# A GNN kernel on one core: the sum of a graph's two slot sums made by POOL in SBUF instead of by two accumulating transposes on TensorE

## What is computed

```python
h = jnp.maximum(_layernorm(x, axis=-1), 0.0)
mask = (adj > 0.0)
h_pair = relu((h @ W1a)[:, :, None, :] + (h[:, :, None, :] - h[:, None, :, :]) @ W1b + b1)   # 192 wide
hm = einsum('bjkh,bjk->bjh', h_pair, mask)
x = x + hm @ W2 + deg[..., None] * b2
h = jnp.maximum(_layernorm(x, axis=-1), 0.0)
x = x + einsum('bno,...->bno', einsum('bnm,bmf->bnf', adj, h), W)
```

## Time and profile before

| | |
|---|---|
| median of 3 runs | 842.6 us (842.23, 842.6, 845.79) |
| the profiled execution | 845.98 us |
| its span, first to last instruction | 844.1 us |
| mean granted TensorE clock | 0.98 |
| PE busy | 810.6 us (96%) |
| DVE busy | 809.9 us (96%) |
| ACT busy | 794.9 us (94%) |
| POOL busy | 611.5 us (72%) |

### The profile page before, as it was taken

How to read it: one execution, slowest core, us unless ns; L and a number is a source line. 1 busy time by engine, 2 the same in 40 slices (tenths; PEclk the granted TensorE clock), 3 DMA queues, 4 the chain that set the end, 5 groups by cost and what they waited for, 6 DMA issues and landing times.

```text
span 844.1 us, 26648 instructions
## 1 busy us (share of the span) xinstructions
PE 810.6 (96%) x8242; PEld 715.0 (85%) x8243; DVE 809.9 (96%) x2894; ACT 794.9 (94%) x2246; POOL 611.5 (72%) x1174
## 2 busy tenths in 40 slices
PE   4879999999999999999999999999999999999996
PEld 2447888898889888988998899888988898889884
DVE  6969999999999999999999999999999999999993
ACT  4969999999999999999999999999999999999992
POOL 1966777777777777777777777777777777777762
PEclk8979999999999999999999999999999999999996
DMA  9800000000000000000000000000000000000000
GB/s 337 327 1 2 7 9 21 21 21 15 21 20 21 9 21 21 20 15 21 21 21 9 20 21 21 15 21 20 21 9 21 21 20 14 21 21 21 15 3 21
DMA packets 26705, 27.55 MB, mean 33 GB/s; under 512 B 3520, under 2 KB 24512, under 8 KB 25536
## 3 DMA queue, kind: packets, MB, share of 16 engines
q1 hardware_dynamic: 25488, 25.37, 8.9%
q10 hardware_dynamic: 1072, 0.43, 0.2%
HBM read 21.59 MB, written 4.19 MB: 31 GB/s over the span
## 4 chain that ended last, share of the span: by engine, by line
PE 90%; DVE 4%; issue 2%; ACT 2%; DMA 1%; SPq 0%; ACTq 0%; DVEq 0%
PE ring L414 48%; PE ring L442 8%; PE prep L471 5%; PE post L514 4%; PE post L501 3%; PE post L508 3%; PE post L502 3%; PE prep L479 3%; PE prep L482 2%; PE prep L477 2%; DVE acc L826 2%; PE post L506 2%; DMA x_all<-x_nbf_dram 1%; PE prep L473 1%; DVE onehot_space L812 1%
## 5 line engine op out<-in xcount | busy, mean ns | idle before, releaser
L826 DVE SCALAR_TENSOR_TENSOR acc<-ring,acc 128x384 f32<-128x384 f32 x896 | 488.6, 545 | 0.6
L572 ACT COPY ring<-P 128x384 f32<-128x384 f32 x1024 | 466.6, 509 | 19.3 <-DVE acc L826 11.4
L414 PE MATMUL ring<-PQ,onehot_space 128*128 128x192 f16 x4096 | 417.0, 247 | 4.5 <-ACT ring L572 2.2
L414 PEld LDWEIGHTS ring<-PQ,onehot_space 128*128 128x128 f16 x4096 | 328.0, 99 | 39.4 <-issue 13.5
L922 POOL TENSOR_SCALAR start<-P,spare 128x192 f32<-128x192 f32 x128 | 128.4, 1003 | 134.8 <-ACT P L622 133.8
L946 POOL TENSOR_TENSOR row_space<-row_space 128x192 f32<-128x192 f32 x256 | 153.4, 599 | 25.3 <-ACT row_space L610 8.2
L812 DVE TENSOR_SCALAR onehot_space<-mask_all 128x512 f16<-128x512 f16 x512 | 158.1, 311 | 0.0
L442 PE MATMUL ring<-PQ,owner 128*128 128x384 f16 (+1 forms) x512 | 93.9, 306 | 0.0
L414 PE MATMUL ring<-PQ,onehot_row 128*128 128x192 f16 x768 | 84.3, 246 | 0.5 <-DVE onehot_row L874 0.3
L610 ACT ACTIVATE row_space<-ring 128x576 f32<-128x576 f32 x128 | 83.3, 651 | 0.7 <-PE ring L414 0.7
L826 DVE SCALAR_TENSOR_TENSOR acc<-ring,start 128x384 f32<-128x384 f32 x128 | 71.1, 556 | 5.3 <-PE ring L414 1.3
(11 more groups left out here) (138 smaller groups left out, 1431.9 us busy)
## 6 DMA issues: line engine op xcount, KB each, us to landing
onehot_space<-adj_kbj_dram SPq DMA_DIRECT2D x8, 1024.0 KB, 17.3
adj_again<-adj_kbj_dram SPq DMA_DIRECT2D x128, 64.0 KB, 2.0
x_all<-x_nbf_dram SPq DMA_DIRECT2D x8, 512.0 KB, 19.0
out_dram<-x_all SPq DMA_DIRECT2D x32, 128.0 KB, 1.9
consts<-consts_dram SPq DMA_DIRECT2D x1, 192.0 KB, 2.4
scratch<-w1a_dram ACTq DMA_DIRECT2D x2, 48.0 KB, 4.2
scratch<-w1b_dram ACTq DMA_DIRECT2D x2, 48.0 KB, 6.7
scratch<-b_dram ACTq DMA_DIRECT2D x1, 96.0 KB, 10.1
```

The lines of the kernel that those rows point to most:

```text
L414: last = nc.tensor.matmul(to, hot(s), parts[:, part, H:2 * H], start=False, stop=(part == 1), skip_group_check=True)
L572: return nc.scalar.copy(slots[to][:, bank_], src.unsqueeze(1).broadcast_to([N, PER_BANK, H]))
L826: return nc.vector.scalar_tensor_tensor(sums, slots[to][:, bank_], 0.0, start[:, :, :] if first else sums, ALU.max, ALU.subtract if first ...
```

## The change

POOL adds the two halves of acc of graph b - 1 in place, into half 0, one tensor_tensor of 128x192 f32 with two inputs in SBUF, and raises a new semaphore, acc_ready. It stands in POOL's stream behind the bias of even steps (L939) or the norm of odd ones (L985), and ahead of the wait for relu_row_ready and the two row adds. It waits for summed, the last consume of the graph. PE waits for acc_ready beside its two other waits and then transposes half 0 alone: one L501 instead of two in each step, one L506 instead of two in even steps. The looped branch keeps both transposes and gets no add.

```diff
--- before.py
+++ after.py
@@ -240,6 +240,7 @@
         loop_gathered = sem("loop_gathered")
         loop_half_summed = sem("loop_half_summed")
         loop_summed = sem("loop_summed")
+        acc_ready = sem("acc_ready")
         half_row_ready = sem("half_row_ready")
         hm_row_ready = sem("hm_row_ready")
         even_T_ready = sem("even_T_ready")
@@ -497,12 +498,14 @@
                             pe.wait_ge(hm_row_ready, b)
                             if not main:
                                 pe.wait_ge(even_T_ready, pairs(b, u, t, -2))
-                            for s in range(PER_BANK):
+                            if not looped:
+                                pe.wait_ge(acc_ready, b)
+                            for s in range(PER_BANK if looped else 1):
                                 nc.tensor.matmul(head_ps, acc_space[:, (u - 1) // 2 % 2, s, heads[(u - 1) % 2]], ident, start=(s == 0), stop=False, is_transpose=True)
                             last = nc.tensor.matmul(head_ps, row_heads[(u - 1) % 2], ownerT[:, (u - 1) % QUAD, :], start=False, stop=True)
                         if u % 2 == 0 and exists(b - 2):
                             k = (u - 2) % QUAD
-                            for s in range(PER_BANK):
+                            for s in range(PER_BANK if looped else 1):
                                 nc.tensor.matmul(tail_ps, acc_space[:, k // 2, s, tails], ident, start=(s == 0), stop=False, is_transpose=True)
                             for g in range(2):
                                 last = nc.tensor.matmul(tail_ps, row_tails[g], ownerT[:, k + g, :], start=False, stop=(g == 1))
@@ -937,6 +940,11 @@
                                             deg[:, of].unsqueeze(2).broadcast_to([N, 2, F]), ALU.mult).then_inc(bias_ready, 1)
                     wait_apart(pool, bias_ready, pair)
                     nc.gpsimd.tensor_tensor(x_all[:, of, :], x_all[:, of, :], bias[:, :, :], ALU.add).then_inc(xb_ready, 1)
+                if exists(b - 1) and not looped:
+
+                    pool.wait_ge(summed, b * REGULAR)
+                    sums = acc[(u - 1) % QUAD]
+                    nc.gpsimd.tensor_tensor(sums[:, 0, :], sums[:, 0, :], sums[:, 1, :], ALU.add).then_inc(acc_ready, 1)
                 if exists(b - 1):
 
                     pool.wait_ge(relu_row_ready, b)
```

## The result

| | before | changed |
|---|---|---|
| median | 843.04 us | 889.32 us |
| the profiled execution's span | 844.1 us | 886.0 us |
| ratio (95% interval) | | 1.0537 (1.0519 to 1.0555) |
| pair of steps, from the row relu's first and last start | 12.04 us | 12.76 us |

The forecast was 861.0 with a range of 836 to 873: the right direction, less than half of the loss. In the changed kernel the lines of the code stand three further down on DVE and ACT: L812 is L815, L865 is L868, L874 is L877, L610 is L613, L826 is L829; on POOL L946 is L954, L959 is L967, and L947 is the new add. The row relu's row (duration in ns, first and last start in us) gives the pace, to be set beside the earlier trace rows: (872.1 - 61.8)/63.5 = 12.76 us a pair, 0.72 more, and 0.72 x 63.5 = 45.9 us is the whole loss (the medians differ by 46.3).

A forecast was written before the change was run, and what follows sets the result against it. It took DVE in even steps and TensorE in odd ones to set the 12.04 us pair of steps; +0.40 from (d) and -0.11 from (a) gave +0.29 us a pair, +18.4 us in all, so 861.0 us, range 836 to 873.

The forecast's parts named there:

- The loop named: DVE through the even step, its last consume releasing ACT's seeds, then TensorE through the odd step; 12.04 us a pair.
- the 0.17 us to spare: DVE's slack in the odd step: its wait for TensorE's gather of the next graph, 0.37 us where 0.20 is needed.
- (a): TensorE: one transpose fewer in odd steps gains 0.11 us a pair, 7.0 us; the even step's 0.22 counts nothing.
- (b): POOL: the new add takes 0.59 us and moves the row adds by 0.55; POOL's own time is free.
- (c): TensorE's wait for the moved row adds: 0 to 0.2 us in odd steps, gone if DVE is 0.4 late.
- Rivals 1 and 2: 1: no costly collision, TensorE waits for row adds, 842 us, chance 0.20; 2: neither collision nor wait, 835.6, 0.23.
- (d): Even steps: two-input POOL adds that start first hold DVE's instructions until they end, costing 0.40 us a pair.
- first kind of even step: Row adds, moved later, hold from_first (L865) by 0.27 us and the onehot (L812) by 0.10, together 0.37.
- The bound from above: Upper limit of DVE's loss to POOL's adds in the even step: two hits, 0.8 us, against 0.40 taken.
- second kind of even step: The new add starts 0.04 us ahead of onehot L812 and holds it, costing 0.41 us.
- the double hit: Slower still than one hit: two hits in one even step of two, 874 us; part of the slow bound of 873.
- port theory: Part (d) as the experiments call it: a POOL instruction in SBUF holds one of DVE's that comes after it.

The follow-up runs named there:

- e1: Kernel before with one head and one tail transpose instead of two and no add on POOL (second slot half left out of the sum); 842.6 us.
- e10: Changed kernel with POOL's new add over 2 of the 192 columns, same instructions, waits and transposes; 837.3 us.
- e6: Changed kernel with POOL's rest part of PQ made to wait until DVE's one-hot rows are done; 911.9 us.
- e8: Changed kernel with the two row adds waiting in every step until DVE is past chunk 1's first consume, new add still ahead of them; 875.1 us.
- e13: Changed kernel with POOL's two-input rest part of PQ made a one-input tensor_scalar of the same size and place; 880.8 us.
- e3: Changed kernel with POOL's new add and two row adds made one-input tensor_scalars of the same size in the same places; 877.8 us.
- e5: Kernel before plus POOL's add of the 128 head columns in odd steps only, saving one head transpose in these; 838.8 us.
- e9: As the odd-step head-column add, but in even steps instead, ahead of the row adds, with equal POOL work and transposes saved; 901.0 us.
- e2: Kernel before with POOL's add in the change's place, written to a tile nobody reads; TensorE keeps all transposes and waits for the add; 892.3 us.
- e12: Head columns added in odd steps ahead of the row adds; 256 columns, tails included, in even steps behind them; all the change's transposes saved; 845.1 us.
- e4: Changed kernel with POOL's new add behind the two row adds instead of ahead of them; 860.4 us.
- e11: Head columns added in odd steps ahead of the row adds and in even steps behind them, one head transpose per step, tails keep both; 847.8 us.

## Why the prediction was right or wrong

**What bounds the kernel.** The loop named, DVE in the even step and TensorE in the odd one, was half of it. e1 shows the other half: in the odd step POOL's first row add let DVE go no sooner than it ended, and the earlier trace rows showed it (L812 at 401.75 ends 0.14 us after the add). The prediction had read this row as a proof of the hold and not as part of the loop. It also took one odd step for all: in 29 of 63 the hold is the longer one and DVE doesn't wait for TensorE, so that the 0.17 us to spare are there in half of them only.

**(a) TensorE's 0.11 us a pair, 7.0 us.** Wrong, as a gain by itself: e1 gives 842.6. In the sum it did no great harm, which was luck: the odd step did become 0.07 us shorter, but through other terms. The hold of chunk 1's onehot and the wait for TensorE are gone, and the one-hot rows (0.53 us instead of 0.38 to 0.40) and chunk 3's onehot (0.38 instead of 0.28) now meet POOL's L925 and L967. With the new add cut to two columns (e10) the same saving together with the moved phases is worth 0.14 us a pair.

**(b) POOL's add, 0.59 us and a shift of 0.55.** Right: 439.50 to 440.11 is 0.61 from start to start, a bit more since the add is held up by DVE for a moment itself (0.64 us long).

**(c) TensorE's wait for the row adds.** It was said to vanish once DVE is late, and it did: counted from the step's first consume, the row adds of odd steps start after 1.16 us instead of 1.40 or 1.64, for all the add ahead of them, and TensorE waits for POOL in the last graph only. Rivals 1 and 2 are out. In e6 and e8, where POOL is held back, this wait comes back with its price.

**(d) DVE against POOL, 0.40 us a pair.** This is the step that failed, by the size of its term. The mechanism, the place and the first meeting were right: in its first kind of even step the prediction had from_first held by 0.27 us and the onehot behind it by 0.10. From start to start the changed kernel has 440.24 to 440.66, 0.42 against 0.13 before, so 0.29, and 441.13 to 441.43, 0.30 against 0.20, so 0.10. What was mis-sized is the number of meetings. DVE, late by 0.4 us against ACT and so against POOL's rest part, met that one with its one-hot rows: 443.22 to 443.98 is 0.76 us where three one-hots need 0.30, so 0.46 more. The prediction followed the delay into the odd step, where it helps, and not to the one-hot rows later in the same step. With 0.46 the even step comes to 0.85 instead of 0.40; measured are 0.82 in the mean of the run. e13 shows that this part is POOL's. The bound from above, two hits or 0.8 us, was nearly right, but for two hits of another kind. The second kind of even step, in which the new add was to hold a onehot, did not occur: nearly all even steps before last 6.01 to 6.18 us, in the changed kernel nearly all 6.96 or 6.97. That the meetings lock the engines' phases is my reading of it; no run tests it.

**The signs.** L865 (L868 now) lasts 0.5 us in even steps, DVE is full, and TensorE and ACT show new waits for it: as forecast. POOL's busy share in the window was to be about 85% and is 78.6, in part since the pair it is a share of has grown.

**The rule of the Trainium skill** on the shared port ("SBUF — State Buffer", Who interferes with whom) said "fully blocks" and made no difference between one input and two. On the first count the trace agrees in the rows shown: from_first at 440.24 ends 0.04 us after the row add that began before it. On the second count I set one row against it, and that was too strong: e3 and e13 show one-input instructions lengthening DVE's, though not holding them to their end. By the Trainium skill's page, from_first at 434.30 in e3 would last until the one-input instruction from 434.27 ends, about 0.7 us with its shortest length of 0.68; it has 0.36. The Trainium skill's page ties the lock to DVE instructions in its 2-port modes or with two SBUF inputs, and no row here shows a mode. What the runs show is who holds whom, when and for how long; that a port is the reason rests on the Trainium skill.

**The range.** The upper end of 873 had the double hit in it only in one even step of two. Both hits in each even step (0.8 us, the upper bound of (d)) give 0.8 - 0.11 = 0.69 us a pair, 843 + 43.8 = 886.8; that bound was worked out and should have been in the range.

## What to carry to other kernels

Before work is moved from a full engine to one with time to spare, look at what the two share, and lay the new instruction's start beside each instruction of the other engine on the same port: two kernels with equal work on POOL and TensorE differ here by 62 us (e5 and e9). When such a meeting delays an engine, follow the delay to the end of the step and through the next one; the next meeting may be the larger one. Knowing the mechanism was not enough to forecast a time: the port theory's range held in e2, e5 and e12, and missed in e1, e3, e4, e6 to e11 and e13, in several because a cured meeting let the engines drift into others. Read several steps of the trace, since one step can be the rarer kind. The best version here, e5, adds only the head columns, in the steps in which TensorE is late, and is 0.6% faster than before.

## What the runs showed of the hardware

- A POOL instruction with two inputs in SBUF that starts 0.06 us ahead of DVE's f16 tensor_scalar holds it to its own end: in the changed kernel (443.16 and 443.22) the first of three one-hots of 128x128 lasts 0.54 us, and the three together 0.88, where they need 0.38 with no POOL instruction beside them (e6). The same with 0.07 us in e6: 0.67 us instead of 0.28.
- With one input the hold is shorter: 0.36 instead of 0.22 us for from_first (e3), 0.69 for the three one-hots (e13), of which the first lasts 0.34. The changed kernel shows it by itself in odd steps: the three one-hots at 436.47 begin 0.08 us behind the one-input L925 of 0.97 us and take 0.53.
- A DVE instruction that is held shows no idle time in the profile, only a longer record: from 99.6 to 100.0 us busy of 100, in a kernel that is 5.4% slower.
- POOL's record grows when DVE is there first: the new add lasts 0.64 us at 439.50 with a onehot running since 439.34, and 0.59 in e6, where it began first. A wait for the onehot's end (439.69) would have made it 0.78.
